# The last projection moved into the second aggregate, and a self product split in two halves of columns

## What is computed

```python
x = x + gat(relu(layernorm(x)))                      # x1_rows in the kernel
h = relu(layernorm(x))                               # h_rows
def sage(h, W_self, W_neigh, b):
    mean = segment_sum(h[src], dst) * deg_inv[:, None]
    return h @ W_self + mean @ W_neigh + b
h1 = relu(sage(h, W_self0, W_neigh0, b0))            # h1_rows
out = x + sage(h1, W_self1, W_neigh1, b1)
```

## Time and profile before

| What | us |
|---|---|
| median of 3 runs (3247.96 to 3252.14) | 3250.93 |
| profiled execution | 3248.66 |
| its span | 3247.0 |
| first aggregate, 1604 to 2322.4 | 718.4 |
| second aggregate, 2322.4 to 2975.7 | 653.3 |
| projection and end, 2975.7 to 3247.0 | 271.3 |

### The profile page before, as it was taken

One profiled execution on the slowest core, in us unless ns is written; L12 is line 12 of the kernel. 1 busy time (PEld: TensorE's weight loads), 2 busy tenths in 40 slices (PEclk: granted clock), 3 DMA queues, 4 the chain that ended last, 5 costly groups with the idle time before them and its releaser, 6 DMA issues. The chain is left out here.

```text
span 3247.0 us, 84374 instructions
## 1 busy us (share of the span) xinstructions
PE 2693.6 (83%) x29961; PEld 1778.2 (55%) x29961; DVE 2289.9 (71%) x4237; ACT 1176.4 (36%) x2818; POOL 1593.5 (49%) x1558
## 2 busy tenths in 40 slices
PE   5467899779999995899777787888588888888999
PEld 5334555368888884444355555555355555554444
DVE  7796778688878898788467777777466666665333
ACT  5464454398888884444311111111100000000110
POOL 2001232167777773222366667676366666673000
PEclk6688999889999998999878888888699999999999
DMA  2795987289999995777599999999699999998555
GB/s 81 226 312 177 325 308 279 78 308 352 355 353 348 354 359 174 241 221 219 192 372 343 343 338 337 329 338 336 233 371 378 368 351 366 334 373 314 152 151 139
DMA packets 279039, 935.76 MB, mean 288 GB/s; under 512 B 50498, under 2 KB 51502, under 8 KB 278638
## 3 DMA queue, kind: packets, MB, share of 16 engines
q0 software_dynamic: 213408, 709.80, 61.0%
q1 hardware_dynamic: 65230, 220.77, 21.5%
HBM read 864.38 MB, written 130.54 MB: 306 GB/s over the span
## 5 line engine op out<-in xcount | busy, mean ns | idle before, releaser
L1823 PE MATMUL gagg_sum_ps<-gagg_got,gagg_hot_hi 128*128 128x256 f16 x3320 | 573.8, 273 | 62.3 <-DVE sums_acc L1769 27.5
L2224 POOL DMA_INDIRECT agg_got<-h_rows,all_win_idx x440 | 469.4, 1067 | 233.2 <-issue 117.3
L1868 POOL DMA_INDIRECT agg_got<-h_rows,all_win_idx x440 | 435.4, 990 | 247.9 <-PE agg_sum_ps L1833 123.1
L1724 POOL DMA_INDIRECT gagg_got<-xs_rows,all_set_idx x415 | 461.9, 1113 | 168.4 <-issue 85.4
L1789 ACT ACTIVATE gagg_hot_hi<-gagg_hot,all_mem 128x128 f16<-128x128 f16 x1660 | 507.0, 387 | 82.0 <-DVE gagg_hot L1742 79.4
L1823 PE MATMUL gagg_sum_ps<-gagg_got,gagg_hot_lo 128*128 128x256 f16 x1660 | 453.6, 273 | 0.0
L1899 DVE TENSOR_TENSOR sums_acc<-agg_sum_ps,sums_acc 128x512 f32 x440 | 304.4, 692 | 173.9 <-PE agg_sum_ps L1833 170.2
L2288 DVE TENSOR_TENSOR sums_acc<-agg_sum_ps,sums_acc 128x512 f32 x440 | 304.1, 691 | 165.2 <-PE agg_sum_ps L1833 159.0
L2332 PE MATMUL agg_out_ps<-agg_w,all_mem 128*128 128x512 f16 x1200 | 349.0, 420 | 63.4 <-issue 54.8
L1833 PEld LDWEIGHTS agg_sum_ps<-all_mem,agg_got 128*128 128x128 f16 x7040 | 280.0, 103 | 188.9 <-issue 98.0
L1833 PEld LDWEIGHTS agg_sum_ps<-agg_hot,agg_got 128*128 128x128 f16 x7040 | 259.0, 100 | 219.7 <-DMA agg_got<-h_rows,all_win_idx 160.7
(11 more groups left out here) (398 smaller groups left out, 3982.3 us busy)
## 6 DMA issues: line engine op xcount, KB each, us to landing
gatw_piece<-slot_rows POOLq DMA_DIRECT2D x52, 512.0 KB
split_w<-edg_w_out SPq DMA_DIRECT2D x32, 512.0 KB, 7.4
agg_got<-h_rows,all_win_idx POOLq DMA_INDIRECT x880
x_rows<-fin_val POOLq DMA_DIRECT2D x25, 500.0 KB
h_rows<-fin_h POOLq DMA_DIRECT2D x25, 500.0 KB
out_dram<-neigh_rows POOLq DMA_DIRECT2D x24, 500.0 KB
norm_x_sb<-in_x_dram SPq DMA_DIRECT2D x25, 448.0 KB
fin_x_sb<-in_x_dram SPq DMA_DIRECT2D x25, 448.0 KB
```

What stands on the lines that cost most here:

```text
L1724: g.indirect_dma_start(out=got[:, u % R, :], out_offset=None, in_=rows_in[:, :], in_offset=bass.IndirectOffsetOnAxis(ap=set_idx[:, col:col ...
L1823: last = t.matmul(sum_ps[g % 2][:, h * C:(h + 1) * C], hot_k[:, u % HOTS, h, :], got[:, u % R, part * D + h * C:part * D + (h + 1) * C], s ...
L1868: g.indirect_dma_start(out=got[:, u % R, :], out_offset=None, in_=rows_in[:, :], in_offset=bass.IndirectOffsetOnAxis(ap=win_idx[:, u:u + 1 ...
L2224: g.indirect_dma_start(out=got[:, u % R, :], out_offset=None, in_=rows_in[:, :], in_offset=bass.IndirectOffsetOnAxis(ap=win_idx[:, u:u + 1 ...
```

## The change

The three stages become two. In `first_layer` (R = 7) PE also makes one half (columns 0 to 511) of the self product of the last layer: the rows of tile i-2, which the kernel still holds as `out16`, are turned before the window at n = 1, moved by ACT behind its high part, and multiplied with two matmuls behind each product piece at n = 3 to 14; DVE reads the half at n = 15, and SP stores it (`part1_rows` is now 512 columns wide). The relu is made in place and its high part copied from it. Behind the last visit come the half products of tiles 23 and 24.

In `last_layer` (R = 7) PE makes the other half (columns 512 to 1023) beside the visits of the same tile, three matmuls behind each window at n = 7 to 14, and the neighbour product of tile i-1 at n = 2 to 13, as in the first layer. DVE adds `x1_rows`, `part1_rows` and the bias at n = 5 and the half product with it (`add_self`); at n = 14 it adds the neighbour product, and SP stores the output and then loads the next rows. `project` is gone. The seventh row buffer, the turned rows and the rows of a tile lie in `mem`, in which the tables of the attention layer lay before.

```diff
...
+        def half_products(half_ps, a_t, w_half):
+            made = [(a_t[:, pa, k, :], w_half[:, k, pw, :]) for k in range(KT) for pa, pw in ((0, 0), (0, 1), (1, 0))]
+            return [(half_ps[:, :], l, r, n < 1, n >= len(made) - 1) for n, (l, r) in enumerate(made)]
...
+        def first_layer(tag, flat, sums, mem):
...
-                R = 9
+                R = 7
                 SUMS = 3
...
                 PIECES = 12
+                TURN_AT, SELF_AT, PART_AT = 1, 3, 15
...
+                    def store_part(j):
+                        tile = tile_reg_at(mybir.EngineType.SP, j)
+                        sp.wait_ge(part_ready, j + 1)
+                        for a, b in CUTS:
+                            sp.dma_start(part1_rows[ds(tile * TN + a, b - a), :], part[a:b, :]).then_inc(part_stored, 16)
...
+                        if n == PART_AT and i >= 2:
+                            read_part(i - 2)
...
+                    low(NT - 1)
+                    read_part(NT - 2)
+                    read(NT - 1)
+                    out_low(NT - 1)
+                    read_part(NT - 1)
...
+                        a.activation(as_turned(a_t, 0), by_feature(sums, tile), ACT.Copy, scale=sum_up[:, 0:1]).then_inc(hi_done, 1)
+                        if j >= 1:
+                            move(j - 1)
...
+                        a.activation(rows[:, :], rows[:, :], ACT.Relu, scale=h1_up[0:TN, 0:1]).then_inc(relued, 1)
+                        a.wait_ge(relued, j + 1)
+                        if j >= 1:
+                            a.wait_ge(turned, j)
+                            a.wait_ge(stored, CUT * j)
+                        a.activation(out16[0:TN, 0:D], rows[:, :], ACT.Copy).then_inc(out_hi, 1)
...
+                        if i >= 2 and n == TURN_AT:
+                            turn(i - 2)
...
+                        if MULTIPLY_AT <= n < MULTIPLY_AT + PIECES and i >= 1:
+                            multiply(i - 1, n - MULTIPLY_AT)
+                        if SELF_AT <= n < SELF_AT + PIECES and i >= 2:
+                            multiply_self(i - 2, n - SELF_AT)
+                    turn(NT - 2)
+                    for piece in range(PIECES):
+                        multiply_self(NT - 2, piece)
+                    for piece in range(PIECES):
+                        multiply(NT - 1, piece)
+                    turn(NT - 1)
+                    for piece in range(PIECES):
+                        multiply_self(NT - 1, piece)
+        def last_layer(tag, flat, sums, mem):
...
+                R = 7
...
+                LO_AT, MULTIPLY_AT, ADD_AT, DONE_AT = 0, 2, 5, 14
+                PIECES = 12
+                SELF_AT, SELF_PIECES = 7, 8
...
+                    def load_more(j):
+                        tile = tile_reg_at(mybir.EngineType.SP, j)
+                        for a, b in CUTS:
+                            sp.dma_start(rows[a:b, :], x1_rows[ds(tile * TN + a, b - a), :]).then_inc(x1_loaded, 16)
+                            sp.dma_start(more[a:b, 0:HALF], part1_rows[ds(tile * TN + a, b - a), :]).then_inc(part_loaded, 16)
...
+                        if i + 1 < NT:
+                            sp.wait_ge(turned, i + 1)
+                            load_row(i + 1)
+                        if i >= 1:
+                            tile = tile_reg_at(mybir.EngineType.SP, i - 1)
+                            sp.wait_ge(out_ready, i)
+                            for a, b in CUTS:
+                                sp.dma_start(out[ds(tile * TN + a, b - a), :], rows[a:b, :]).then_inc(stored, 16)
+                            sp.wait_ge(stored, CUT * i)
+                            load_more(i)
...
+                    def add_self(j):
+                        v.wait_ge(x1_loaded, CUT * (j + 1))
+                        v.wait_ge(part_loaded, CUT * (j + 1))
+                        v.wait_ge(bias_loaded, 16)
+                        v.tensor_tensor(rows[:, :], rows[:, :], more[0:TN, :], ALU.add).then_inc(mixed, 1)
+                        v.wait_ge(mixed, j + 1)
+                        v.wait_ge(self_done, j + 1)
+                        v.scalar_tensor_tensor(rows[:, HALF:D], half_ps[0:TN, :], post_self[:, 0:1], rows[:, HALF:D], ALU.mult, ALU.add).then_inc(self_read, 1)
...
+                        if n == ADD_AT and i >= 1:
+                            add_self(i - 1)
+                        if n == DONE_AT and i >= 1:
+                            tile = tile_reg_at(mybir.EngineType.DVE, i - 1)
+                            v.wait_ge(self_read, i)
+                            v.wait_ge(prod_done, i)
+                            v.scalar_tensor_tensor(rows[:, :], out_ps[0:TN, :], post[:, ds(tile, 1)], rows[:, :], ALU.mult, ALU.add).then_inc(out_ready, 1)
...
                         a.activation(as_turned(a_t, 0), by_feature(sums, tile), ACT.Copy, scale=sum_up[:, 0:1]).then_inc(hi_done, 1)
...
+                        if j + 1 < NT:
+                            move(j + 1)
...
                     for u, (i, n) in enumerate(place_of):
+                        if n == 0:
+                            turn(i)
...
                         if MULTIPLY_AT <= n < MULTIPLY_AT + PIECES and i >= 1:
                             multiply(i - 1, n - MULTIPLY_AT)
...
+                        if SELF_AT <= n < SELF_AT + SELF_PIECES:
+                            multiply_self(i, n - SELF_AT)
+                    ready(NT - 1)
+                    todo = products(out_ps, a_t, w16)
+                    for q, done in enumerate((half_done, prod_done)):
+                        for o, l, r, start, stop in todo[q::2]:
+                            last = t.matmul(o, l, r, start=start, stop=stop)
+                        last.then_inc(done, 1)
...
-            neighbours("agg0", h_rows, NEIGH0, part0_rows, h1_rows, flat, sums, mem)
-            sums_and_product("agg1", h1_rows, flat, (SELF1, b1, part1_rows))
-            project("neigh1", NEIGH1, out, sums, (part1_rows, x1_rows))
+            first_layer("agg0", flat, sums, mem)
+            last_layer("agg1", flat, sums, mem)
...
```

More of the change, by code:

```diff
@@ L145, in powers @@
         step(v.tensor_scalar(up.bitcast(i32), power, -1.0, float((254 + TOP) << 23), ALU.mult, ALU.add))
[L147 to L177, removed]
     top = ExitStack()
@@ new lines, in _ @@
+                    for k in range(1, R, 2):
+                        v.memset(got[k].bitcast(f32), 0.0).then_inc(blank[1], 1)
+                        if k < AHEAD:
+                            make_hot(k - 1)
+                            make_hot(k)
+                    v.memset(out16[:, :], 0.0).then_inc(cleared, 1)
+                    for u, (i, n) in enumerate(place_of):
+                        at = at_reg(mybir.EngineType.DVE, u)
+                        if u + AHEAD < VISITS:
+                            make_hot(u + AHEAD)
+                        v.wait_ge(mm_done, u + 1)
+                        if u >= 1:
+                            v.wait_ge(added, u)
+                        v.tensor_tensor(window_of(flat, at), sum_ps[u % SUMS][:, :].rearrange("p (k d) -> p k d", k=KT), window_of(flat, at),
+                                        ALU.add).then_inc(added, 1)
+                        if n == LO_AT and i >= 1:
+                            low(i - 1)
+                        if n == READ_AT and i >= 1:
+                            read(i - 1)
+                        if n == PART_AT and i >= 2:
+                            read_part(i - 2)
+                        if n == OUT_AT and i >= 1:
+                            out_low(i - 1)
@@ L2295, in _ @@
                     v.wait_ge(added, VISITS)
                     low(NT - 1)
-                    read(NT - 1)
-                    out_low(NT - 1)
+                    add_self(NT - 1)
+                    tile = tile_reg_at(mybir.EngineType.DVE, NT - 1)
+                    v.wait_ge(self_read, NT)
+                    for q in range(2):
+                        cols = slice(q * HALF, (q + 1) * HALF)
+                        if q == 0:
+                            v.wait_ge(half_done, 1)
+                        else:
+                            v.wait_ge(prod_done, NT)
+                        v.scalar_tensor_tensor(rows[:, cols], out_ps[0:TN, cols], post[:, ds(tile, 1)], rows[:, cols], ALU.mult, ALU.add).then_inc(half_ready, 1)
@@ L2304, in _ @@
+                    move(0)
                     for j in range(NT):
```

580 lines of the change are left out of this document (249 added, 331 removed).

## The result

The changed kernel takes 3407.38 us (median of 4 runs, 3391.46 to 3412.86) against 3249.44 us (4 runs) for the one before: the ratio is 1.0477, with an interval of 1.0441 to 1.0513. The forecast was 3226 us with a range up to 3290, so both the sign and the size were wrong. The profiled execution has a span of 3404.8 us, 157.8 us more than before.

The account below looks back on a forecast made before the run. It took the first aggregate as bound by PE's dense part plus a chain, the second by DMA, the projection by TensorE. 137.7 + 91.7 - 251.9 = -22.5 us on 3248.66 gave 3226 us, range 3165 to 3290.

Parts of the forecast that it names:

- The end: Behind the last addition: 19.4 us remain of 271.3, so 251.9 us go.
- The first layer: First aggregate with half the self product added: 5.0 us more per tile, 115 for 23 tiles, +137.7 us with its ends.
- start and tail: First layer's ends: 5.8 us to load half weights, 16.9 us of work behind the last visit.
- the half product's 4.75 us: First layer, per tile: 24 more matmuls take 5.2 us, of which 4.75 lengthen PE's dense part.
- The second rival: First layer: turn and longer dense part keep the clock from falling, 55 us less, 3171 us; chance 0.18.
- I take 29.0; the ends are 27.5 and 32.: Last layer: microseconds per tile against 25.5 before, 84 us over 24 tiles, +91.7 us with the start.
- The third rival: Last layer: add_self at n = 5 waits for x1 rows; 2 us late costs 34 us, 3260 us; chance 0.12.
- Nothing here: First layer: seven row buffers in place of nine add no time; PE's wait for gathered rows was 11.0 us.
- DMA side, 28.5 us: Last layer, per tile: gathers 22.0 us plus 3.5 transfers at 6.5 us.
- The first rival: Last layer held by row buffers and falling clock together: 32 us per tile, 3298 us; chance 0.22.
- PE's 27.5: Last layer, PE's time per mean tile: 20.5 us of dense work, then the chain at 7.0.
- chain of 7.0 us: Last layer's tile end: 9.17 us before, less out_low and its wait and 0.4 additions, leaves 7.0.

Follow-up runs that it names:

- e4: e1 with the first layer's turn at n = 3 instead of 1 and its half product at n = 6 to 13; 3334.74 us, ratio 1.0257.
- e1: Changed kernel, last layer's half product read out at n = 5 without waiting for rows, which are added at n = 13; 3275.85 us, ratio 1.0084.
- b7: Kernel before the change with seven row buffers in both aggregates instead of nine and eight; 3292.54 us, ratio 1.0131.
- e8: e6 with six row buffers in the last layer instead of seven; 3235.51 us, ratio 0.9946.
- e5: e1 with 14 of the last layer's 24 half-product matmuls moved to the tile boundary; 3254.31 us, ratio 0.9998.
- e2: Changed kernel without the x1 and part1 row loads behind the first tile; 3263.25 us in one run.
- e7: e6 with the last layer's three loads of a tile asked for at n = 7; 3215.98 us, ratio 0.9880.
- e6: e5 with all 24 first-layer half matmuls in the boundary, turn at n = 3, half read at n = 5; 3191.30 us, ratio 0.9802.

## Why the prediction was wrong

**The end** was right: 252.5 us went, 251.9 were forecast.

**The first layer** was 33 us too dear. Its start and tail came to 104.6 - 23 x 3.54 = 23.2 us (forecast 22.7), but a tile grew by 3.5 us and not by 5.0. The sum had the half product's 4.75 us in the dense part and nothing given back. Read off the trace of PE for 23 tiles, the dense part, from the first to the last of a tile's groups of four product matmuls, grew from 16.95 to 19.55 us, and the time from there to the next product from 10.35 to 11.2. So the dense part grew by only 2.6 us, and the pause by 0.9 where 0.25 was forecast. What was given back is in the rows behind `e4`: in ten of 23 tiles the product starts at full clock, in seven partly so. The second rival named this with 55 us and a chance of 0.18. It came about in part: the pause and the half clock moved ahead of the turn (2.06 us, and 1.89 for 16 transposes).

**The last layer** was the step that failed: "I take 29.0; the ends are 27.5 and 32." It was 37.78, and four things make the difference of 8.8 us a tile.

The largest is the loop, 5.8 us (`e1`). The third rival had this mechanism with its place and slack: a half product that waits for `add_self`, which waits for the x1 rows. It was priced at 34 us and set aside with one sentence, "they are asked for about 9 us before their use". No row stood behind that sentence, neither for the 9 us nor for the time that such a load takes. In the round shown DVE was free for the addition at 2876.05, 6.5 us after the first part was asked for and 4.8 after the last, and the last took 9.6. SP asked only 8 us after the read, because the store ahead of it needed 5.1 us and its issue and waits the rest. Rows late by 2 us were assumed; the wait of DVE was 5.4 us in the mean and 10.1 at most. The Trainium skill ("DMA: Bandwidth & Descriptors", Anatomy of one DMA) gives a transfer that GpSimd issues a fixed 2.0 us and the bytes at 436 GB/s; for 0.75 MB that would be an estimate of 3.7 us. These loads are issued by SyncE and run beside gathers, and the trace has 9.6, which decides.

The next is the seventh buffer. "Nothing here" was said of the first layer and nearly holds (`b7`, 4.5 us in all). But the last layer's DMA side, 28.5 us, was worked out from a stage with eight buffers. With 1.8 us a tile from `b7`, or 2.0 from `e8`, it is 30.3 to 30.5, and `e5`, with a DMA share of 0.99 and most of PE's waits for gathered rows, measured 30.76. The first rival had 1.1 us for it.

The third and the fourth lie on PE's side, and the trace of `e2`, which hardly waits for gathers, has both: 31.23 us for 27.5. PE's 27.5 held no slow restart. By the forecast's terms the first to the last group of the product take 18.5 us; in `e2` they take 20.4, and most of its products start at half clock. And the chain of 7.0 us was too short: from the product group at n = 13 to the next product the terms are 0.86 + 0.65 + 0.47 + 7.0 = 9.0 us, and `e2` takes 10.8 in the mean of 23 tiles. Which part of the chain makes these 1.8 us is open.

So both sides stood above 29.0, PE's at 31.2 and the gathers' at 30.3 to 30.8. Together they made the 31.97 of `e1`, and the loop put 5.8 on top. Of the 214 us that the last layer's visits cost beyond the forecast, the loop has about 139 (24 x 5.8), the two sides about 71 (24 x 2.97), and a start of 11.0 us for 7.7, which is what the sum leaves over, the rest. These shares hold in the order in which the experiments took the causes away; how the 2.97 us fall to buffer, clock and chain can't be told from these runs, since taking away one alone leaves the next just beneath.

The chance of "slower" was 0.25, spread over rivals taken one at a time. They were not alternatives: the loop came on top of buffers and clock in every tile.

What stays open: why the loads beside the gathers take 6 to 11 us, whether they cost less elsewhere (a run with rows asked for early and used later than in `e7` was not made), and what `e6` would take without the wait for its part store.

## What to carry to other kernels

A load whose buffer is freed by a store is a loop: read, store, landing, load, landing, use. Write its sum down with landing times from the same stage, with the same gathers in flight, and compare it with the visits between; a slack counted in the consumer's work is worth nothing without the transfer's time. Where a price comes from a stage with another number of buffers, price the buffer first. And where an engine's clock falls in a pause at each tile, the work to be added belongs in the pause: the same 24 matmuls per tile cost 3.5 us in the dense part and 1.1 us in the boundary. Behind each such move look again for a buffer that waits for its own store: `e6` got a new one.

## What the runs showed of the hardware

A DMA share near 1 does not mean a full rate. One row buffer less, with nothing else changed in the stage, left the share near 1 and lowered the rate: from 1.01 and 363 GB/s to 0.97 and 337 (`b7`), and from 0.99 and 323 (`e6`) to 0.97 and 306 (`e8`). The share counts the time of packets under way. The number of buffers alone does not set the rate: seven gave 337 in `b7`, 323 in `e5` and 311 in `e1`, which differ in what runs beside the gathers.

A load of three quarters of a megabyte by SP landed 6.3 to 11.1 us after its last part was asked for in the boundary (9.6 in the round shown) and, in the one read in mid-tile, after 11.75 us, both beside gathers and a load of 0.5 MB in the same queue.

TensorE's clock at a restart was not the same from tile to tile of one kernel. In the changed kernel's first layer four matmuls of 512 columns took 1.02 to 1.05 us at ten of 23 restarts and 1.86 to 1.89 at six; with six windows and 24 matmuls spread over the pause (`e6`) they took 1.02 at 22 of 23.
